# Spreading the feed-forward pairs of a long round evenly between its scores, in a fused attention and feed-forward kernel

## The reference

```python
xn = layernorm(x)                                  # over the 256 values of a token
# attention, 16 heads of 16 values, with biases
q, k, v = split(xn @ Wq + bq), split(xn @ Wk + bk), split(xn @ Wv + bv)
q, k = rope(q), rope(k)
weights = softmax(einsum('bhnd,bhmd->bhnm', q, k) / sqrt(256))
attn = merge(einsum('bhnm,bhmd->bhnd', weights, v)) @ Wo + bo
# feed-forward: weights are +1 or -1, from booleans k0, k1, k2
h = concat([xn, -xn]); h = 2 * relu(s0 * (h @ sign(k0)))      # 512 -> 1024
h = 2 * relu(s1 * (h @ sign(k1)))                             # 1024 -> 1024
ffn = s2 * (h @ sign(k2))                                     # 1024 -> 256
out = x + attn + ffn
```

## Time and profile before

| | |
|---|---|
| Time, median of 3 runs | 2622.96 us (2622.56 to 2623.35) |
| The profiled execution | 2623.22 us, of which 2621.4 us are the span from its first to its last instruction |
| Mean granted TensorE clock | 0.993 of full speed |
| TensorE matmuls busy | 2573.5 us |
| ScalarE busy | 2083.4 us |
| VectorE busy | 1042.9 us |
| GpSimd busy | 613.1 us |

### The profile page before, as it was taken

How to read it: one execution, slowest core, us unless ns; L and a number is a source line. 1 busy time by engine, 2 the same in 40 slices (tenths; PEclk the granted TensorE clock), 3 DMA queues, 4 the chain that set the end, 5 groups by cost and what they waited for, 6 DMA issues and landing times.

```text
span 2621.4 us, 49554 instructions
## 1 busy us (share of the span) xinstructions
PE 2573.5 (98%) x20711; PEld 1334.0 (51%) x20711; DVE 1042.9 (40%) x1666; ACT 2083.4 (79%) x2310; POOL 613.1 (23%) x429
## 2 busy tenths in 40 slices
PE   7898999999999999999999999999999999999999
PEld 5774454545444454545445454545445454544545
DVE  7974343342434242342424333243424234243423
ACT  5876888888888878787887878787887878787884
POOL 5673212122212222021212213121122202120210
PEclk9998999999999999999999999999999999999999
DMA  8983111111212122121212112121212112121212
GB/s 265 293 265 102 50 55 51 48 51 50 62 52 71 43 71 65 46 67 59 78 48 72 51 60 66 49 75 52 82 44 79 54 48 68 55 78 51 72 39 98
DMA packets 198233, 202.08 MB, mean 77 GB/s; under 512 B 144820, under 2 KB 148732, under 8 KB 191608
## 3 DMA queue, kind: packets, MB, share of 16 engines
q1 hardware_dynamic: 195128, 189.99, 23.5%
q10 hardware_dynamic: 2880, 8.91, 0.9%
HBM read 131.34 MB, written 67.50 MB: 76 GB/s over the span
## 4 chain that ended last, share of the span: by engine, by line
PE 91%; ACT 0%; DVE 0%; issue 0%; DVEq 0%; SPq 0%
PE ps_o L1101 37%; PE ps_f L1134 28%; PE ps_s L1088 24%; PE ps_y L1147 2%; PE ps_s L1183 0%; PE ps_f L1183 0%; ACT probs L1066 0%; DVE probs L1343 0%; PE ps_f L1191 0%; PE ps_o L1183 0%; PE ps_y L1183 0%; PE ps_s L1191 0%; DVEq L870 0%; PE ps_o L1191 0%; PE ps_y L1191 0%
## 5 line engine op out<-in xcount | busy, mean ns | idle before, releaser
L1066 ACT ACTIVATE probs<-ps_s 128x1024 f32<-128x1024 f32 x2048 | 1931.0, 1033 | 451.7 <-PE ps_s L1088 449.6
L1101 PE MATMUL ps_o<-probs,v_ones 128*32 128x512 f32 x8192 | 1011.4, 600 | 0.0
L1088 PE MATMUL ps_s<-q_rows,k_rows 50*128 50x512 f32 x4096 | 864.8, 439 | 4.1 <-SPq L1038 3.0
L1088 PEld LDWEIGHTS ps_s<-q_rows,k_rows 50*128 50x128 f32 x4096 | 364.4, 184 | 671.8 <-ACT probs L1066 594.5
L1234 POOL TENSOR_TENSOR heads<-heads,sums 128x512 f32<-128x512 f32 x64 | 82.3, 1287 | 1870.1 <-DVE sums L1262 1870.1
L1101 PEld LDWEIGHTS ps_o<-probs,v_ones 128*32 128x32 f32 x8192 | 200.7, 108 | 418.3 <-issue 295.8
L1134 PE MATMUL ps_f<-h_hi,ffn_w 64*128 64x512 f32 x2048 | 406.3, 392 | 0.0
L1134 PE MATMUL ps_f<-h_lo,ffn_w 64*128 64x512 f32 x2048 | 406.1, 392 | 0.0
L1286 DVE COPY raw<-ps_f 128x512 f32<-128x512 f32 x256 | 164.9, 686 | 560.1 <-PE ps_f L1134 560.0
L1262 DVE RECIPROCAL sums<-sums 128x128 f32<-128x128 f32 x256 | 226.6, 924 | 1.7
L1297 DVE SCALAR_TENSOR_TENSOR h_lo<-raw,h_hi 128x512 fp32r<-128x512 f32 x256 | 216.2, 844 | 8.7
(11 more groups left out here) (128 smaller groups left out, 1608.4 us busy)
## 6 DMA issues: line engine op xcount, KB each, us to landing
k_rows<-k_parts SPq DMA_DIRECT2D x128, 256.0 KB
q_rows<-q_heads SPq DMA_DIRECT2D x384, 64.0 KB
k_parts<-parts SPq DMA_DIRECT2D x32, 512.0 KB, 4.8
k_rows<-k_parts SPq DMA_DIRECT2D x128, 128.0 KB
x_chunk<-in_x ACTq DMA_DIRECT2D x16, 512.0 KB, 6.1
xn_d<-xn_t SPq DMA_DIRECT2D x16, 512.0 KB, 5.7
q_heads<-parts SPq DMA_DIRECT2D x32, 256.0 KB, 6.7
v_heads<-v_sb SPq DMA_DIRECT2D x16, 512.0 KB, 5.8
```

The source lines that it names most:

```text
L1066: nc.scalar.activation(probs[:, s % PBUF, half * 2 * C:(half + 1) * 2 * C], ps_s[:, half].rearrange("p c n -> p (c n)"), ACT.Exp, scale=SC ...
L1088: last = nc.tensor.matmul(ps_s[:, half, w], k_rows[rows, u, t * P:(t + 1) * P], q_rows[rows, u, half], start=True, stop=True)
L1101: last = nc.tensor.matmul(ps_o[32 * c:32 * c + 2 * DH], v_ones[:, u, t], probs[:, s % PBUF, c * C:(c + 1) * C], start=(t == 0), stop=(t == ...
```

## The change

Before, a long round gave its pairs to three visits, behind the first, second and third score: 4, 2 and 2 pairs in FIRST, 3, 3 and 2 in SECOND, 6, 5 and 5 in THIRD. The fourth score was followed at once by the two weighings. Now there are four visits of 2 pairs (of 4 in THIRD), one behind each of the four scores; the last one stands between the fourth score and the weighings. The number of pairs in a round, their order, and the round in which a group of pairs ends stay the same. No instruction is added or taken away.

```diff
-VISITS_PER_ROUND = ((4, 2, 2), (3, 3, 2), (6, 5, 5))
+VISITS_PER_ROUND = ((2, 2, 2, 2), (2, 2, 2, 2), (4, 4, 4, 4))
...
-        n = 3 if count == 2 else 0
+        n = 4 if count == 2 else 0
         out.append(left[:n])
```

## The result

| | before | changed |
|---|---|---|
| Time, median of 4 runs | 2623.15 us (2622.56 to 2624.15) | 2788.04 us (2787.25 to 2789.47) |
| Span of the profiled execution | 2621.4 us | 2786.1 us |
| Mean granted TensorE clock | 0.993 | 0.994 |

The changed kernel is slower: 1.0628 times the time of before (95% interval 1.0615 to 1.0642), 165 us more. The forecast was 2798, within 2765 to 2830.

A forecast was written before the change was run, and what follows sets the result against it. TensorE and ScalarE hold one another up, the fourth score waiting for exponentials; pairs moved behind it add 10.9 us a pass, 175 over 16 passes, to 2623.2: 2798.2, less 0.3 for the median, 2798 us, range 2765 to 2830.

The forecast's parts named there:

- What bounds the kernel: TensorE and ScalarE hold one another up; in a long round the fourth score comes almost exactly when its half is free.
- Round behind a short one: Long round after a short one: fourth score stays at 2.71, round 5.46 against 5.00, +0.47 us, 16 rounds a pass.
- Round behind a long one: Long round after a long one: fourth score at 2.55, round 5.30 against 4.86, +0.45 us, 7 rounds a pass.
- the one in FIRST: The eighth long round behind a long one, in FIRST: earlier scores help, 5.30 against 5.05, +0.25 us a pass.
- The sum: All long rounds of a pass: 16 x 0.47 + 7 x 0.45 + 0.25 = 10.9 us, 175 us over 16 passes.
- The bounds: Over 384 long rounds: 2761 us if the fourth score's wait cost no loading ahead, 2833 if the changeover cost twice 0.09.
- VectorE and the queues: VectorE's copies of finished groups keep 0.66 us of room, and DMA loads come later with everything else: nothing taken.
- 1: Faster: fourth score no longer held, rounds behind a short one drop from 5.00 to 4.86, 36 us less, 2587; 2%.
- 2: No change: waits at the second to fourth score vanish in the 594.5 us weight loads already wait, 2623; 2%.
- 3 (partly hidden): Exponentials follow more closely or a held score costs under 0.11: 0.1 to 0.36 us a round, 2661 to 2761; 8%.
- 4 (the clock): Three held scores a round lower TensorE's clock; one 7.46 us round a pass adds 38 us, 2837; 2%.
- What the changed profile was to show: Rounds of 5.4 to 5.5 and 5.3 us, second to fourth scores held, ScalarE idle 610 to 625 us, clock 1.00.

## Why the prediction was right

**What bounds the kernel.** Right. The held fourth score at 2.71 behind a short round was taken from the earlier trace rows as a time that ScalarE sets. It stood at 2.71 in the kernels with one, two and three pairs behind it, and at 2.20 as soon as the exponentials were halved.

**Round behind a short one.** The single times came out: second score 0.87 (0.90 forecast), third 1.79 (1.81), fourth 2.71 (2.71), weighings 3.60 (3.60), round 5.46 (5.46). The first two came a little early because the 0.07 us between an exponential's end and the score was mis-sized. It is 0.05; the exponential that frees the fourth score takes 1.05 instead of 1.03, and the two errors cancelled there. The changeover from a 512-column pair to the weighings, which no row of before showed, took 1018.03 - 1017.71 = 0.32 (0.325 forecast). The term of 0.47 fits the 184 rounds of SECOND and THIRD. It was too large in two kinds that had not been told apart. The rounds of FIRST behind a short one took 5.07 before, as their four pairs in the first gap held the fourth score to 2.78 there too, so they lost only 0.39; the prediction had seen this for the round behind a long one alone. And where a projection (1.92 us) stretches the short round ahead, ScalarE has nothing in hand, and the round behaves as one behind a long one: 4.87 before, 5.29 with the change, 0.42.

**Round behind a long one.** Forecast 5.30, measured 5.29 on average; before, 4.86. The difference is 0.43, where the prediction had rounded 5.30 - 4.86 = 0.44 up to 0.45. For the one in FIRST it is 5.29 - 5.06 = 0.23 (0.25 forecast).

**The sum.** 10.9 us a pass forecast, 10.3 measured; 175 us and 165. Of the 10 us too many, about 4 are FIRST behind a short round, 3 the rounds behind a long one and 1 the projections; the rest is smaller. The largest of these errors is a length of before, read from one round of SECOND where FIRST differed.

**The bounds.** The lower one took the 0.11 of lost loading off all 384 rounds. Most rounds behind a short one had paid that 0.11 before the change as well, so it could bear on little more than a third of them. Nothing came to hang on it, as the loss of loading was there in full.

**VectorE and the queues.** Taken at nothing, and nothing appeared: in the changed kernel no round is more than 0.03 us over the mean of its kind, those behind a group's end included.

**Rivals.** 1 and 2 (the fourth score no longer held, or the waits hidden) are refuted by the same row at 2.71. 3 (partly hidden) by the same rows, and by the experiments with one and three pairs: each pair costs nearly its 0.235. 4 (the clock) by the granted clock of 1.00 over a pass with two or three held scores in every long round. Its price was too low besides: the round of 7.46 us had a mean granted clock of 0.61, and was at the lower level only for its first 5.8 us.

The Trainium skill (TensorE: Matmul & The Clock Gate, "A second HAM failure mode: psum-queue depth-cycling") tells of a kernel in which short idle moments between groups of matmuls made the clock swing. This case did not go that way: with holds of about 0.1 us the clock stayed at 1.00 through the passes.

**What the changed profile was to show.** ScalarE's idle time is 1.51 us behind a long round and 626.8 us in all (1.5 and 610 to 625 forecast, so just over). The second score behind a long round is not held, as its working said (0.80) but not the summary at the end, which had all three held.

## What to carry to other kernels

When two engines feed each other through two buffers, find in the timeline the one instruction of a round that is held, and what frees it. Work ahead of it is free up to the moment at which it is freed; work behind it and ahead of the next round is paid nearly in full (here 0.21 to 0.23 us of the 0.235 of a pair), so an even spread is not a neutral one. Filler belongs ahead of the last hand-over, sized so that it arrives just when the buffer is free; and the price of an order is best taken as a mean over all rounds of its kind.

## What was unexpected in the hardware

That a short hold costs more than its wait stands in the prediction, for one round. Two rows of the kernel before show how: the weight loads of the fourth score, first held, then in the round of the earlier trace rows, where the score itself was not late.

```profile
1013.82 0.18 PEld L1088 LDWEIGHTS ps_s<-q_rows,k_rows 50*128 50x128 f32 x2 [0.30 <-ACT probs L1066]
```
```profile
1007.16 0.19 PEld L1088 LDWEIGHTS ps_s<-q_rows,k_rows 50*128 50x128 f32 x2 [0.16 <-ACT probs L1066]
```

The held one starts with its matmul, at 1013.82; the other 0.11 ahead of its matmul at 1007.27. What was unexpected is how much it adds up to. In the kernel before, the fourth score was held in 247 of the 382 long rounds, 0.50 us long instead of 0.40. With nothing held, a long round fell from 4.96 to 4.87 us on average, so this pattern cost about 33 us of the kernel before.
